# Second expert layer regrouped by unordered pairs of experts, 128 rows to a group, written straight to the output

## What is computed

```python
logits = xf @ gate_w + gate_b
probs = jax.nn.softmax(logits, axis=-1)
top2_vals, top2_idx = jax.lax.top_k(probs, 2)
cw = jnp.zeros((N, Ee), dtype=xf.dtype).at[jnp.arange(N)[:, None], top2_idx].add(top2_vals)
def step(acc, params):
    w1, bb1, w2, bb2, we = params
    h = jax.nn.gelu(xf @ w1 + bb1, approximate=False)
    y = h @ w2 + bb2
    return (acc + we[:, None] * y, None)
...
x = x + _L1_ffn_ref(_layernorm(x, axis=-1), ...)
```

## Time and profile before

| | |
|---|---|
| median of three runs | 972.79 us |
| the profiled execution | 966.81 us, span 965.0 us |
| busy share | PE 69%, DVE 78%, POOL 57%, ACT 50% |
| mean granted clock of TensorE | 0.823 of full speed |
| the chain that ended last | PE 26%, issue 22%, POOL 21%, DVE 21%, DMA 5% |
| DMA | 111.51 MB, mean 116 GB/s |

### The profile page before, as it was taken

The page is one execution under the profiler, slowest core; times in us unless marked ns, Lnnn a source line. Parts: engine busy times, 40 slices in busy tenths (PEclk is TensorE's granted clock), DMA queues, the critical chain, the costliest instruction groups (busy, mean ns, idle before and its releaser), DMA issues.

```text
span 965.0 us, 24021 instructions
## 1 busy us (share of the span) xinstructions
PE 662.5 (69%) x6281; PEld 552.2 (57%) x6282; DVE 753.1 (78%) x2881; ACT 479.1 (50%) x1065; POOL 546.6 (57%) x544
## 2 busy tenths in 40 slices
PE   3977677450999999998078878777208778778400
PEld 2755455350999999998066667666206656556300
DVE  6699999661899999998469989997517777787468
ACT  2466655410777777775146656664206555555200
POOL 0027777765376666767100666666664777777700
PEclk9998989755999999999568777777558998998755
DMA  8283333232233322326524544332333333333899
GB/s 223 81 198 105 104 103 109 75 113 59 67 94 86 86 82 85 87 78 173 142 59 134 140 131 140 89 89 68 93 92 93 99 102 100 97 101 98 224 237 285
DMA packets 168828, 111.51 MB, mean 116 GB/s; under 512 B 30306, under 2 KB 157737, under 8 KB 168776
## 3 DMA queue, kind: packets, MB, share of 16 engines
q1 hardware_dynamic: 151496, 77.04, 30.6%
q0 software_dynamic: 17280, 33.87, 10.6%
HBM read 60.32 MB, written 52.36 MB: 117 GB/s over the span
## 4 chain that ended last, share of the span: by engine, by line
PE 26%; issue 22%; POOL 21%; DVE 21%; DMA 5%; ACT 2%; SPq 1%; POOLq 1%; DVEq 0%; ACTq 0%
POOL row_buf L448 16%; PE bank L616 10%; PE bank L630 9%; POOL y_buf L456 5%; DVE xin L941 4%; DVE stat L886 3%; DVE x1w L993 2%; PE bank L602 2%; DMA y_buf<-g_y,g_dst 2%; PE bank L511 1%; DMA yin<-y_buf 1%; PE bank L528 1%; ACT xn L691 1%; DVE x1w L941 1%; PE bank L515 1%
## 5 line engine op out<-in xcount | busy, mean ns | idle before, releaser
L448 POOL DMA_INDIRECT row_buf<-pay,slot x256 | 255.2, 997 | 235.3 <-DVE slot L1062 155.8
L456 POOL DMA_INDIRECT y_buf<-g_y,g_dst x284 | 291.2, 1025 | 137.2 <-issue 89.9
L616 PE MATMUL bank<-g_xT,w 128*128 128x256 f16 x1278 | 171.4, 282 | 1.5 <-ACT g_xT L795 1.0
L795 ACT ACTIVATE g_xT<-bank 128x512 f16<-128x512 f16 x142 | 84.8, 597 | 170.0 <-PE bank L602 168.1
L616 PEld LDWEIGHTS bank<-g_xT,w 128*128 x1278 | 120.2, 101 | 21.0 <-issue 2.6
L602 PE MATMUL bank<-ident,g_in 128*128 128x128 f16 x568 | 58.3, 228 | 84.4 <-DMA g_in<-row_buf 71.7
L630 PE MATMUL bank<-w,g_h 128*128 x1260 | 86.3, 222 | 18.1 <-DVE g_y L1210 18.1
L802 ACT ACTIVATE xn<-bank,b_cols 128x256 f32<-128x256 f32 x216 | 86.7, 473 | 22.0 <-PE bank L616 15.5
L630 PEld LDWEIGHTS bank<-w,g_h 128*128 128x128 f16 x1260 | 77.8, 99 | 26.9 <-issue 24.7
L802 ACT ACTIVATE xt<-bank,b_cols 128x256 f32<-128x256 f32 x210 | 84.2, 474 | 16.1 <-PE bank L616 12.8
L602 PEld LDWEIGHTS bank<-ident,g_in 128*128 128x128 f16 x568 | 38.2, 102 | 92.4 <-issue 75.7
(11 more groups left out here) (184 smaller groups left out, 1363.0 us busy)
## 6 DMA issues: line engine op xcount, KB each, us to landing
g_in<-row_buf SPq DMA_DIRECT2D x142, 130.0 KB, 2.2
yin<-y_buf SPq DMA_DIRECT2D x24, 512.0 KB, 6.6
x_buf<-x1w SPq DMA_DIRECT2D x16, 520.0 KB, 4.5
xin<-x_buf SPq DMA_DIRECT2D x10, 520.0 KB, 5.6
y_buf<-g_y,g_dst POOLq DMA_INDIRECT x284
xin<-in_x_dram SPq DMA_DIRECT2D x8, 512.0 KB
adj_in<-in_adj_dram SPq DMA_DIRECT2D x16, 256.0 KB
row_buf<-pay,slot POOLq DMA_INDIRECT x256, 2.4
```

Of the source, the lines that this page charges most:

```text
L448: pool.indirect_dma_start(row_buf[L][:, :], bass.IndirectOffsetOnAxis(ap=slot[q][:, k, t:t + 1], axis=0), pay[q][:, t, :], None).then_inc( ...
L456: pool.indirect_dma_start(y_buf[L][:, :], bass.IndirectOffsetOnAxis(ap=g_dst[k][:, t:t + 1], axis=0), g_y[k][:, t, :], None, bounds_check= ...
L616: last = nc.tensor.matmul(dst, w[:, bass.ds(e * (2 * HID[L]) + (wp * HID[L] + c * P), P)], g_xT[q][:, xp, :], start=(m == 0), stop=(m == 2))
L795: nc.scalar.activation(g_xT[q][:, :, :], x_ps[q], ACT.Copy).then_inc(s.gT_sb, 1)
```

## The change

The first layer keeps its groups. In the second:

- A token is put once into the list of its unordered pair of experts (28 pairs) instead of once into each of two lists. `route_pairs` sums a power of two per chosen expert and compares with 28 codes; the rank tables have 28 columns per tile, not 8. The row is 1040 bytes: the 520 of before, then the two weights in the pair's order and the residual row in fp32. There are 8 indirect DMAs per block, not 16, and no store to `x1_buf`.
- Groups have 128 rows of one pair; there are 91. `pair_tables` makes the tables; a TensorE matmul brings them to one row.
- Per group TensorE does 2 transposes, 12 up matmuls of 128 columns (two experts, two chunks, three products), and down products for two experts: one fp16 matmul of a bias row each and two matmuls in fp32 each, on the rows as gelu wrote them; VectorE's split is gone. `w2f` holds the second matrix in fp32.
- VectorE multiplies each expert's result by its weight, adds the residual, and GpSimd writes 128 finished rows straight to the output with one indirect DMA. The last stage is gone.
- SyncE loads eight groups ahead. TensorE reads its two expert numbers in two reads of one value for each group; ScalarE in two reads of eight values per eight groups.
- The padding of the second layer's lists is written in advance: 28 x 128 rows of 1040 bytes in place of 1792 rows of 520 bytes. `pair_constants` on VectorE is new, between `split_first(0)` and `groups(0)`. The second layer's `split_second` is gone.

```diff
-                    for LL in range(2):
-                        sp.dma_start(row_buf[LL][NE * CAP:ROWS, :].rearrange("(t p) w -> p t w", p=P),
-                                     pad_row[:, :].unsqueeze(1).to_broadcast([P, SPARE // P, ROW_W])).then_inc(spare_out, 16)
+                    sp.dma_start(row_buf[0][NE * CAP:ROWS, :].rearrange("(t p) w -> p t w", p=P),
+                                 pad_row[:, 0:ROW_W].unsqueeze(1).to_broadcast([P, SPARE // P, ROW_W])).then_inc(spare_out, 16)
+                    sp.dma_start(row_buf[1].rearrange("(l c) w -> c l w", c=CAPP)[0:PG, :, :],
+                                 pad_row[:, :].unsqueeze(1).to_broadcast([P, PAIRS, WIDE_W])).then_inc(spare_out, 16)
...
+                def load_next(g, k):
+                    sp.wait_ge(s.gT_ps, g + 1)
+                    sp.wait_ge(s.y_ready, g + 1)
+                    load_group(g + DEEP, k)
...
-                        for k in range(TOP):
+                        for k in range(TOP if L == 0 else 1):
                             for t in range(TILES):
                                 pool.indirect_dma_start(
                                     row_buf[L][:, :], bass.IndirectOffsetOnAxis(ap=slot[q][:, k, t:t + 1], axis=0),
-                                    pay[q][:, t, :], None).then_inc(s.scattered[q], 16)
+                                    pay[q][:, t, :] if L == 0 else row[q][:, t, 0:WIDE_W], None).then_inc(s.scattered[q], 16)
...
+                        pool.indirect_dma_start(
+                            out[:, :], bass.IndirectOffsetOnAxis(ap=p_dst[k][:, 0:1], axis=0),
+                            p_out[k], None, bounds_check=N_TOK - 1, oob_is_err=False).then_inc(s.y_out[k], 16)
...
+                def experts(g):
+                    return [table_values(mybir.EngineType.PE, pair_tab[0:1, k, :], g, 1, NE - 1)[0] for k in range(2)]
+
+                def up(g, k, es):
+                    wait_past(pe, s.act_done, g - 3)
+                    pe.wait_ge(s.gT_sb, g + 1)
...
+                    for m, e in enumerate(es):
+                        for c in range(NC[1]):
...
+                            for j, (wp, xp) in enumerate(((0, 0), (0, 1), (1, 0))):
+                                last = nc.tensor.matmul(dst, w[:, bass.ds(e * (2 * HID[1]) + (wp * HID[1] + c * P), P)],
+                                                        p_xT[k % 2][:, xp, :], start=(j == 0), stop=(j == 2))
...
+                def down(g, k, es):
...
+                    wait_past(pe, s.y_ready, g - 1)
+                    pe.wait_ge(s.act_done, g + 1)
+                    for m, e in enumerate(es):
...
+                        nc.tensor.matmul(dst, sh_row[:, :], b2_row[:, bass.ds(e * D, D)], start=True, stop=False)
+                        for c in range(NC[1]):
+                            last = nc.tensor.matmul(dst, p_act[k % DEEP][:, m * NC[1] + c, :], w[:, bass.ds(e * (NC[1] * D) + c * D, D)],
+                                                    start=False, stop=(c == NC[1] - 1))
...
+                    for k in range(n):
+                        g = DEEP * i + k
+                        if not last or k + 3 < n:
+                            to_feature_rows(k + 3, i)
+                        if not last or k + 2 < n:
+                            es.append(experts(g + 2))
+                            up(g + 2, k + 2, es[k + 2])
+                        down(g, k, es[k])
...
+                def gelu(g, k, es):
+                    act.wait_ge(s.h_ps, g + 1)
+                    for m, e in enumerate(es):
+                        for c in range(NC[1]):
+                            at = m * NC[1] + c
+                            last = nc.scalar.activation(p_act[k % DEEP][:, at, :], bank[k % 4][:, at * PG:(at + 1) * PG], ACT.Gelu,
+                                                        bias=vec_cols[:, bass.ds(e * NC[1] + c + V_B1P, 1)], scale=1.0 / (S_X * S_W))
...
+                    ch.did(V.scalar_tensor_tensor(p_y[a], y[:, 0:D], rows[:, ROW_W:ROW_W + 1], rows[:, ROW_W + X_AT:WIDE_W], ALU.mult, ALU.add))
+                    V.tensor_tensor(p_dst[a][:, :], rows[:, D:D + 1], twice[:, bass.ds(g, 1)], ALU.add)
+                    ch.wait()
+                    V.scalar_tensor_tensor(p_out[a], y[:, D:2 * D], rows[:, ROW_W + 1:ROW_W + 2], p_y[a], ALU.mult, ALU.add).then_inc(s.y_ready, 1)
...
-            for n in range(NBLK):
-                dve.wait_ge(fin_in[n], 48)
-                add_experts(fin_x[n], fin_y[n % len(fin_y)]).then_inc(fin_done, 1)
```

More of the change, by code:

```diff
@@ L37 @@
 NO_TOKEN = 4 * N_TOK
+PAIRS = NE * (NE - 1) // 2
+PG = P
+NGP = N_TOK // PG + PAIRS - 1
+CAPP = N_TOK + PG
+WIDE_W = ROW_W + X_END
+FULL_W = ROW_W + TILE_W
+DEEP = 8
 AHEAD = 4
@@ L348, in step @@
                         load_x(L, n + 2, q)
-                    if not isinstance(n, int) or n >= 1:
+                    if L == 0 and (not isinstance(n, int) or n >= 1):
                         store(L, n - 1, (q + 1) % 2)
@@ new lines, in _ @@
+            blocks(0)
+            pe.wait_ge(stage_in, 32)
+            for e in range(NE):
+                for c in range(NC[0]):
+                    k = e * NC[0] + c
+                    last = nc.tensor.matmul(bank[0][:, k:k + 1], w_stage[:, e * HID[0] + c * P:e * HID[0] + (c + 1) * P],
+                                            vec_cols[:, V_B + e:V_B + e + 1], start=True, stop=True)
+            last.then_inc(bw_ps, 1)
+            groups(0)
+            blocks(1)
+            pair_groups()
@@ L828, in groups, with pair_groups, copy_x, experts @@
                 turn(TURNS, last=True)
-            for L in range(2):
-                blocks(L)
-                groups(L)
+            def pair_groups():
+                s = SL[1]
+                x_ps = [bank[b][:, 0:PG].bitcast(F16).rearrange("p (h n) -> p h n", h=2) for b in (4, 7)]
+                def copy_x(g, q):
+                    act.wait_ge(s.gT_ps, g + 1)
+                    nc.scalar.activation(p_xT[q], x_ps[q], ACT.Copy).then_inc(s.gT_sb, 1)
+                def gelu(g, k, es):
[5 more added lines that the diff above has]
+                                                        bias=vec_cols[:, bass.ds(e * NC[1] + c + V_B1P, 1)], scale=1.0 / (S_X * S_W))
+                    last.then_inc(s.act_done, 1)
+                def experts(g, n):
+                    return [table_values(mybir.EngineType.Activation, pair_tab[0:1, k, :], g, n, NE - 1) for k in range(2)]
+                load_table(ACT.Gelu)
+                act.wait_ge(s.tables, 1)
+                for k in range(2):
+                    copy_x(k, k)
+                ea, eb = experts(0, 2)
+                gelu(0, 0, (ea[0], eb[0]))
+                copy_x(2, 0)
+                gelu(1, 1, (ea[1], eb[1]))
+                def turn(i, last=False):
+                    n = PAIR_TAIL - 2 if last else DEEP
+                    ea, eb = experts(DEEP * i + 2, n)
+                    for k in range(n):
+                        if not last or k < n - 1:
+                            copy_x(DEEP * i + k + 3, (k + 1) % 2)
+                        gelu(DEEP * i + k + 2, k + 2, (ea[k], eb[k]))
+                with act.Fori(0, PAIR_TURNS) as i:
+                    turn(i)
+                turn(PAIR_TURNS, last=True)
+            blocks(0)
+            groups(0)
+            blocks(1)
+            pair_groups()
         @block.vector
@@ L1250 @@
+            blocks(0)
+            V.memset(h_sb[:, :, H_END:H_END + 1], 1.0)
+            ch.did(V.tensor_copy(tok_run[:, :], cst[:, C_TOK:C_TOK + TILES]))
+            group_tables(0)
+            split_first(0)
+            pair_constants()
+            groups(0)
+            blocks(1)
+            pair_tables()
+            split_first(1)
+            pair_groups()
 _INS = ['x', 'adj', 'L0_gnn_W', 'L0_gnn_a_src', 'L0_gnn_a_dst', 'L0_ffn_Wr', 'L0_ffn_br', 'L0_ffn_ln_g', 'L0_ffn_ln_b',
```

422 lines of the change are left out of this document (295 added, 127 removed).

## The result

The changed kernel takes **1032.05 us** (median of 4 runs, 1029.19 to 1034.21) against 972.4 (971.42 to 972.97) beside it: ratio 1.0613, 95% interval 1.0580 to 1.0645. It is **slower by 6%**, and outside the range given. The profiled execution has a span of 1032.4 us, 67.4 over the 965.0 of before.

The account below looks back on a forecast made before the run. TensorE was taken to bound layer 0's groups, and POOL's indirect DMAs layer 1's. The terms -44.4 - 14.9 + 5 + 7 + 24.7 = -22.6 on 966.8 gave 944.2 profiled, times 1.0062: 950 us, range 912 to 993.

Parts of the forecast that it names:

- The last stage: The stage behind layer 1's groups, 920.6 to 965.0 us, goes whole: -44.4 us.
- The scatters of layer 1's blocks: Eight instead of sixteen per block on POOL, cost taken by rows, so layer 1's groups start earlier: -14.9 us.
- rival 4: Scatters on POOL: half as many, but 1040 bytes cost double, so no gain there; 965 us, chance 0.06.
- The blocks of layer 1: VectorE bounds them and gets wider operations, 0.7 us a block over eight blocks: +5 us, ends 0 and +8.
- The padding: More pad bytes delay block 3's input in layer 0, and VectorE stops for it: +7 us, ends 0 and +12.
- The groups: Layer 1's 91 groups at 2.35 us plus 7.7 for filling and draining, 221.6 against 196.9 us: +24.7.
- TensorE's instruction queue: Per group of layer 1, reads, matmul issue and addresses: 2.1 us with reads at 0.277, 2.8 at 0.551.
- T: Time of one of layer 1's 91 new groups: 2.35 us, ends 2.05 and 2.8.
- break-even: Time per group of layer 1 at which the change neither gains nor loses: 2.60 us.
- Rival 2: TensorE's queue stops for its reads between transposes and up product, 0.55 us each: 991 us, over 973 to 1000, chance 0.22.
- T near 2.9: Time per group of layer 1 if the skill's 600 ns floor held: 1.5 us of reads a group.
- Rival 3: Waits in each of layer 1's groups keep TensorE at half clock, 1.2 GHz: 1082 us, chance 0.04.

Follow-up runs that it names:

- e11: Two fp32 matmuls of 384 columns, results unused, before a turn's reads, against the version with gathered, aligned reads and spread padding (955.72 us): 953.51 us.
- e12: Three such unused fp32 matmuls before a turn's reads instead of two, against the same version with gathered, aligned reads and spread padding: 953.99 us.
- e4: The changed kernel with the down product's fp32 matmuls made fp16, on columns of the first matrix: 1030.47 us, one run.
- e3: The changed kernel with TensorE reading both experts of ten groups in two reads per eight groups, instead of 20 one-value reads: 974.07 us.

## Why the prediction was wrong

- **The last stage**, -44.4: right. **The scatters of layer 1's blocks**, -14.9: measured -14.4. By rows, not by bytes, so rival 4 falls.
- **The blocks of layer 1**, +5: +6.2. **The padding**, +7 with ends 0 and 12: 11.3 us when layer 1 begins in this profile, and some 6 over the ten that share its layer 0, of which spreading the padding recovered half. The stop was there as said (4.84 us). Not forecast was the granted clock behind it, 0.67 from 60 to 120 us, where it was 0.94 before (first row below: changed, second: before). These four terms sum to -47.3 in the forecast and to -41.3 in the trace. The -44.4 counted the end of the program as gone with the stage; it came back behind the groups, below.

```profile
60.00:120.00 60.00, 49.92 (x273) 38.34 (x274) 45.60 (x237) 30.00 (x67) 38.24 (x38) 0.67 0.50 141
```

```profile
60.00:120.00 60.00, 44.22 (x315) 32.03 (x315) 55.56 (x292) 37.15 (x83) 42.55 (x42) 0.94 0.38 112
```

- **The groups**, +24.7: measured +108.7. This is the term that failed, and within it the line "TensorE's instruction queue". The array was right (1.96 against 1.89). The queue's sum was put at 2.1 us, the 2.5 reads of an average group included, and is 3.23 (2.91 inside a turn, with two reads). Step by step: the **addresses**, "some 16" at 0.3 together, cost 1.34 for 14; the **reads**, 2.5 at 0.277 = 0.69, cost 0.93 for two and 1.16 for 2.5, 0.465 each with the address work and the silence around a duration of 0.30; the **issue**, 1.1 for 26 passes, is too high, 0.73 for the 24 that there are, with waits and the loop's branch. So the addresses alone, 1.0 us a group too cheap, are more than the whole miss of T, and the reads' 0.5 and the issue's 0.4 nearly cancel. The duration of a read was put right by SyncE's row and not by TensorE's 0.551, which was of two values.
- A small duration was the trap. No row of before gave a price to an address instruction beside a matmul, because layer 0's 256-column matmuls keep the array busy far longer than the queue. The prediction should have given that term ends of its own, as it did for the reads.
- The edge of a turn was put at 2 us, for ScalarE's reads, and costs 2.6, for TensorE's. With it the average group is 3.23 us, where 2.60 was the break-even. The end was too short as well: 11.3 us from TensorE's last matmul (1021.1) instead of 3.6, of which 8.4 are behind the last scatter, and 7.4 of these are GpSimd's DRAIN behind the last bytes, which no term of the sum had. 91 x (3.23 - 2.35) = 80, and 7.7 for the end, less the 4.1 of filling that the 3.23 holds, make the 84 us by which the groups miss their forecast.
- **Rival 2**, TensorE's queue, was the right place, and had 0.22. Its price (0.55 us a read) and its condition (from 0.47 us a read) were not what decided: at 0.465 a read it would have stood at its break-even; the addresses took it to 1032, past the 1000 at which it ended.
- The Trainium skill, DMA: Bandwidth & Descriptors, section "Latency and other measured facts", gives a tensor_load a floor of about 600 ns. The trace does not agree: it has 295 ns as the shortest of 230 one-value reads on TensorE and 302 as the median. The T near 2.9 that it gave in the prediction lies nearer to the measured 3.23 than 2.35 does, but by luck: it was made of reads of 0.6 us, and the cost is mostly the addresses'.
- **Rival 3**, half clock: the granted clock of the changed kernel's groups was 0.88 to 0.93, and e11 and e12 show for the gathered version that even this part was nearly free. The Trainium skill, TensorE: Matmul & The Clock Gate, section "A second HAM failure mode: psum-queue depth-cycling", ties an oscillating clock to small idles between matmul groups. Here it did oscillate, but only behind the gap of a turn's edge; inside a turn of the changed kernel, with 0.28 us of idle in each group, it stayed full. In e4, with 0.5 to 0.9 us of idle in each group, it also fell in the middle of a turn (half level from 874.3 to 881.1 us), so there the trace agrees.

What is open: why the weight load behind an address instruction of 0.046 us starts only 0.096 us after it. The 0.05 between is seen in every trace here and explained by none.

## What to carry to other kernels

Where matmuls are short (128 columns, 0.06 us), add up the instruction queue as carefully as the array: every matmul with its weights, every address that comes from a register (here 0.096 us), every table read (0.45 to 0.50 us for one value). What lies under the array's time costs nothing, and each further tenth of a microsecond is paid once per group. Read tables in a few long, aligned reads outside the inner groups. And before a half-clock stretch is called a loss, look at whether another limit just behind it would have taken the same time. Where GpSimd's indirect DMAs are the last work of a kernel, count its DRAIN behind them (here 7.4 us after the last bytes).

## What the runs showed of the hardware

- A read's duration follows where its values lie. On TensorE: one value 0.30 us, two 0.55, ten from a multiple of eight 1.08, ten from 91 + 8i up to 2.49. On ScalarE: eight from 8i + 2 take 1.77, ten from 8i take 0.99. All four of the long ones touch two stretches of eight aligned values, so the number of stretches alone does not set the time; nor does the place alone, since ScalarE's eight values from 93 + 8i in e3 take 1.77 as well. What does is not shown.
- The compiler drops a read whose value is not used, so a cost probe has to use what it reads.
- An indirect scatter of 128 rows takes POOL 0.96 us for rows of 520 and of 1040 bytes alike.
- GpSimd's DRAIN at the end of the program ends 8.2 us after its last indirect DMA in all fifteen kernels of the change; in the changed kernel that is 7.4 after the last bytes have landed.
- An fp32 matmul of 128 columns takes the array 0.25 us at full clock with both of its passes, and the second pass costs the queue next to nothing (e4).
